# First batch's feed-forward inputs made one tile per attention group and fetched from DRAM, in a two-block adaLN kernel

## The reference, cut to what matters

```
x [4 batches, 512 rows, 512]                       two adaLN blocks
block 0: x = x + ga*attn0(ln(x)*(1+ca)+sa);  x = x + gb*ffn0(ln(x)*(1+cb)+sb)
block 1: x = x + ga*attn1(ln(x)*(1+ca)+sa)         <- "attention groups"
           attn1: 32 query heads of 128, 8 key/value heads, causal in windows of the
           whole sequence, softmax in f32, then @ w_o (4096 x 512)
         x = x + gb*ffn1(h), h = ln(x)*(1+cb)+sb    <- "last stage"
           ffn1(h) = down( silu(gate(h)) * up(h) ), hidden width 1792 = 14 chunks of 128
ln(v) = (v - mean(v)) / sqrt(var(v) + 1e-5), along the last axis (512)
```

## Time and profile before

| | us |
|---|---|
| median of 3 runs | 1852.1 |
| profiled execution, its own time | 1854.24 |
| its span, first to last instruction | 1852.5 |
| PE busy | 1807.5 (98%) |
| DVE busy | 1283.4 (69%) |
| ACT busy | 1123.1 (61%) |
| POOL busy | 448.1 (24%) |
| mean granted TensorE clock | 0.992 |

### The profile page before, as it was taken

One profiled execution on the slowest core, in us unless ns is written; L12 is line 12 of the kernel. 1 busy time (PEld: TensorE's weight loads), 2 busy tenths in 40 slices (PEclk: granted clock), 3 DMA queues, 4 the chain that ended last, 5 costly groups with the idle time before them and its releaser, 6 DMA issues.

```text
span 1852.5 us, 29061 instructions
## 1 busy us (share of the span) xinstructions
PE 1807.5 (98%) x8863; PEld 1508.2 (81%) x8863; DVE 1283.4 (69%) x3032; ACT 1123.1 (61%) x2620; POOL 448.1 (24%) x429
## 2 busy tenths in 40 slices
PE   6998999999999999999999999999999989999999
PEld 4566788888888888888888888888888867888887
DVE  6897677877767676766777777777777785544442
ACT  5755766667667676766666676666666673333331
POOL 2234404041323224041612123140313132010000
PEclk9899999999999999999999999999999999999999
DMA  9026567666766776776776778677777767313010
GB/s 347 2 80 224 157 191 216 203 192 191 204 200 194 211 200 198 205 231 207 214 211 197 208 202 226 191 217 212 197 213 203 210 186 243 109 57 114 27 41 23
DMA packets 239368, 331.25 MB, mean 179 GB/s; under 512 B 26008, under 2 KB 165528, under 8 KB 238880
## 3 DMA queue, kind: packets, MB, share of 16 engines
q1 hardware_dynamic: 238736, 328.93, 59.6%
q10 hardware_dynamic: 528, 1.05, 0.2%
HBM read 200.39 MB, written 129.50 MB: 178 GB/s over the span
## 4 chain that ended last, share of the span: by engine, by line
PE 79%; DVE 7%; DMA 6%; ACT 4%; SPq 2%; issue 2%; DVEq 0%; ACTq 0%
PE ps L2073 23%; PE ps L2139 15%; PE ps L2264 11%; PE ps L2121 9%; PE ps L2106 9%; PE ps L2246 5%; DMA turned_blocks<-tp 4%; ACT probs L2362 2%; PE ps L2125 1%; PE ps L2103 1%; SPq L1779 1%; PE ps L1245 1%; DMA pd<-turned_blocks 1%; DVE pt L2628 1%; DVE stats L864 1%
## 5 line engine op out<-in xcount | busy, mean ns | idle before, releaser
L2073 PE MATMUL ps<-hA,wq 128*128 128x512 f32 x1536 | 385.8, 400 | 0.0
L2139 PE MATMUL ps<-wo,oT 128*128 128x512 f32 x1536 | 367.2, 390 | 3.7 <-issue 2.3
L2139 PEld LDWEIGHTS ps<-wo,oT 128*128 128x128 f32 x1536 | 287.8, 188 | 64.3 <-issue 3.1
L2604 DVE CUSTOM_DVE_ANT_0 ps<-ps,mask 128x512 f32<-128x512 f32 (+3 forms) x512 | 235.8, 523 | 143.5 <-PE ps L2106 142.9
L2381 ACT ACTIVATE pt<-pd 128x1280 fp32r<-128x1280 f32 x128 | 163.0, 1273 | 272.2 <-PE ps L2121 231.3
L2073 PEld LDWEIGHTS ps<-hA,wq 128*128 128x128 f32 x1536 | 279.0, 188 | 56.4 <-issue 0.2
L2362 ACT ACTIVATE probs<-ps,nmax 128x512 f32<-128x512 f32 (+3 forms) x512 | 263.1, 532 | 71.3 <-DVE nmax L2604 71.3
L2370 ACT ACTIVATE probs<-probs,rinv 128x512 f32<-128x512 f32 (+3 forms) x512 | 246.2, 552 | 38.3 <-DVE rinv L2610 38.3
L2121 PE MATMUL ps<-pt,V 128*128 128x512 f32 (+2 forms) x1152 | 253.3, 349 | 11.1 <-DVE pt L2628 10.5
L2121 PEld LDWEIGHTS ps<-pt,V 128*128 128x128 f32 x1152 | 196.2, 190 | 40.3 <-issue 15.3
L2106 PE MATMUL ps<-kT,qT 128*128 128x512 f32 (+2 forms) x1152 | 224.7, 340 | 0.0
(11 more groups left out here) (256 smaller groups left out, 2602.3 us busy)
## 6 DMA issues: line engine op xcount, KB each, us to landing
turned_blocks<-tp SPq DMA_DIRECT2D x128, 640.0 KB, 3.5
pd<-turned_blocks SPq DMA_DIRECT2D x512, 160.0 KB, 3.3
wq_next<-in_L_attn_w_q_dram SPq DMA_DIRECT2D x16, 1024.0 KB, 6.5
wo_in<-in_L_attn_w_o_dram SPq DMA_DIRECT2D x15, 1024.0 KB, 8.2
turned_weights<-hf_chunk SPq DMA_DIRECT2D x168, 64.0 KB, 2.6
wm<-in_L_wmod_dram SPq DMA_DIRECT2D x4, 2048.0 KB, 13.5
turned_values<-tv SPq DMA_DIRECT2D x32, 256.0 KB, 3.2
xh_m<-turned_weights SPq DMA_DIRECT2D x28, 256.0 KB, 3.7
```

Source lines behind the costliest of these rows:

```text
L2073: last = nc.tensor.matmul(ps[:, bank, :], w[i][:, c, cols], hT[k][:, c, b * S:(b + 1) * S], start=(c == 0 and n == 0), stop=(c == DC - 1 a ...
L2139: last = nc.tensor.matmul(ps[:, bank, :], oT[x_][:, b, h, r * P:(r + 1) * P], wo[y_][:, h, :], start=(h == 0 and n == 0), stop=(h == GQ - ...
L2604: nc.vector.tensor_tensor_reduce(out=v, in0=v, in1=mask[:, TB * P - KEYS[i]:], scale=-1.0, scalar=3e38, op0=ALU.add, op1=ALU.min, accum_ou ...
```

## The change

The preparation of batch 0 leaves group 15. In groups 9 to 12, one tile of 128 rows in each, SP loads x and attention of the tile (unit 0), POOL adds them, SP stores the sum to `attended` (unit 1), DVE makes the statistics (unit 2), POOL takes the inverse root with 14 small chained instructions and normalises (in front of its second split of q weights), DVE transposes (unit 4), the bounce goes through DRAM (units 4 and 5), ACT modulates and rounds (unit 6), DVE makes the low part (unit 7), and SP stores both parts to `first_inputs` in DRAM. In group 15 SP loads these into `fT` (units 1, 6, 7), and in flush the sum into `xt[:, 0]`. The loop over groups is cut in two. PE's 16 transposes, ACT's eight modulations, its square root and the table exchange, POOL's copies and DVE's four low parts are gone from group 15 and flush. `gate_up(0, 0)` moves in front of `outputs(g, -1)` and `gate_up(0, 1)` behind it; `place_wide(0)` moves into unit 7 and `place_wide(1)` in front of `p_low(g, -1)`.

```diff
-                    with eng.Fori(NKV + 1, NG - 1) as g:
+                    with eng.Fori(NKV + 1, NKV + 1 + TB) as g:
+                        body(g, False, True, True)
+                    with eng.Fori(NKV + 1 + TB, NG - 1) as g:
                         body(g, False, True)
...                                                          SP: new helpers
+                        def load_ahead(g):
+                            sp.dma_start(hp_f[0], tile_view(mid_t, g)).then_inc(ld_x[PAIR], 16)
+                            sp.dma_start(hp_f[1], tile_view(att_t, g)).then_inc(ld_x[PAIR], 16)
+                        def store_sum(g):
+                            sp.wait_ge(s["root"], ROOT_STEPS * ahead_job(g) + 1)
+                            sp.dma_start(tile_view(att_t, g), hp_f[0]).then_inc(stored, 16)
+                        def store_ahead_turned(g):
+                            sp.wait_ge(n_turned, ahead_job(g) + (AHEAD_JOBS + 1))
+                            sp.dma_start(rows_d.rearrange("a j b x -> (a j) (b x)"), hp_f[1]).then_inc(n_bounced, 16)
+                        def load_ahead_turned(g):
+                            sp.wait_ge(n_bounced, 16 * ahead_job(g) + 16 * (AHEAD_JOBS + 1))
+                            for b_ in range(NQD):
+                                sp.dma_start(hp_f[0][QD * b_:QD * (b_ + 1), :]..., rows_d[:, :, b_, :]...)
+                        def store_ahead(g):
+                            sp.wait_ge(n_lo, ahead_job(g) + (AHEAD_JOBS + 1))
+                            for k in range(2):
+                                sp.dma_start(first_d[k]..., hp_f[k]...).then_inc(later_stored, 16)
+                        def load_first(k, chunks):
+                            sp.dma_start(fT[k][:, chunks, :].bitcast(F32), first_d[k, chunks]...) \
+                                .then_inc(ld_at_first, 16)
...                                                          SP: body
-                                if not more and u < 2:
+                                if not more and u == 1:
                                     sp.wait_ge(wq_split, GQ * NG)
-                                    ...
-                                    sp.dma_start(x_first[:, two, :], mid_t[0][:, two, :])
-                                    for t in range(2):
-                                        sp.dma_start(at_first[t], att_t[0][:, 2 * u + t, :])
+                                    sp.wait_ge(later_stored, 32 * (AHEAD_JOBS + TB))
+                                    load_first(0, slice(1, DC))
+                                    load_first(1, slice(0, 2))
                                 if not more and u >= 6:
                                     for q in range(2 * (u - 6), 2 * (u - 6) + 2):
                                         load_turned(sp, q)
+                                if not more and u == 6:
+                                    load_first(1, slice(2, DC))
+                                if not more and u == 7:
+                                    load_first(0, slice(0, 1))
+                                if ahead and u == 0:
+                                    load_ahead(g)
+                                if ahead and u == 1:
+                                    store_sum(g)
+                                if ahead and u == 4:
+                                    store_ahead_turned(g)
+                                if ahead and u == 5:
+                                    load_ahead_turned(g)
+                                if ahead and u == 7:
+                                    store_ahead(g)
...                                                          SP: flush, behind gsc, usc, dsc
+                            sp.wait_ge(q_full, UNITS * NG)
+                            sp.wait_ge(v_full, PAIR * NG)
+                            sp.dma_start(xt[:, 0], att_t[0]).then_inc(s["x0"], 16)
                             sp.wait_ge(s["w_kept"], 16 * NQD * TILES + 16)
                             next_weights(4)
                             next_weights(5)
...                                                          POOL: normal_ahead, between next_q(0) and next_q(1)
+                            pool.wait_ge(s["agg"], k + 1)
+                            then(nc.gpsimd.tensor_scalar(var, mv_f[:, 0, 1:2], EPS, None, ALU.add))
+                            then(nc.gpsimd.tensor_scalar(root.bitcast(I32), var.bitcast(I32), -0.5, ROOT_SEED, ...))
+                            for _ in range(4):
+                                then(nc.gpsimd.tensor_scalar(step, root, var, root, ALU.mult, ALU.mult))
+                                then(nc.gpsimd.tensor_scalar(step, step, -0.5, 1.5, ALU.mult, ALU.add))
+                                then(nc.gpsimd.tensor_tensor(root, root, step, ALU.mult))
+                            nc.gpsimd.tensor_scalar(hp_f[0], hp_f[0], mv_f[:, 0, 0:1], root, ALU.subtract, ALU.mult)
...                                                          PE
                         def gate_up(n, j, first):
-                            if j == 0:
-                                pe.wait_ge(s["lo"], DC * n + (DC + 2))
+                            if first and j == 0:
+                                pe.wait_ge(ld_at_first, 64)
+                                pe.wait_ge(exp_done, UNITS * TB * NG + TB)
...                                                          PE: flush
                             outputs(g, -2)
-                            pe.wait_ge(s["hi"], DC + 1)
-                            turn(xt[:, 1], range(3, DC))
                             out_project(g - 1, 3)
+                            gate_up(0, 0, True)
                             outputs(g, -1)
+                            gate_up(0, 1, True)
                             out_project(g - 1, 4)
-                            gate_up(0, 0, True)
                             out_project(g - 1, 5)
-                            gate_up(0, 1, True)
                             out_project(g - 1, 6)
                             out_project(g - 1, 7)
...                                                          ACT: body, unit 6, behind p_high
+                                if ahead and u == 6:
+                                    modulate_ahead(g)
...                                                          (four activations of 128x128 and a copy of 128x512)
-                                if last and u == 4:
-                                    root(0)
-                                    nc.scalar.activation(rstd_2[:, TB:TB + 1], rstd_2[:, TB:TB + 1], ACT.Exp, scale=0.0)
...                                                          DVE: body, at the end of the units
-                                if last and u == 6:
-                                    normal(0, lambda t: x_first[:, t, :], xt[:, 1])
-                                if last and u in (2, 3):
-                                    statistics_first(2 * u - 4)
-                                    statistics_first(2 * u - 3)
-                                if last and u == 3:
-                                    variances(0)
+                                if ahead and u == 2:
+                                    statistics_ahead(g)
+                                if ahead and u == 4:
+                                    turn_ahead(g)
+                                if ahead and u == 7:
+                                    low_ahead(g)
+                                if last and u == 7:
+                                    dve.wait_ge(wo_split, GQ * NG)
+                                    place_wide(0)
...                                                          DVE: flush
                             p_low(g, -2)
                             o_low(g, -3)
-                            dve.wait_ge(wo_split, GQ * g)
-                            place_wide(0)
                             add_out(g - 1, 2)
-                            lows(0, range(2))
                             o_low(g, -2)
+                            place_wide(1)
                             p_low(g, -1)
                             add_out(g - 1, 3)
-                            lows(0, range(2, DC))
                             o_low(g, -1)
-                            place_wide(1)
                             add_out(g - 1, 4)
```

170 lines of the change are left out of this document (101 added, 69 removed).

## The result

| | kernel before | changed kernel |
|---|---|---|
| median, us | 1851.8 (4 runs, 1851.4 to 1853.2) | 1877.3 (4 runs, 1874.5 to 1881.0) |
| ratio | 1 | 1.0135 [1.0119, 1.0150] |
| profiled execution, us (span) | 1854.24 (1852.5) | 1874.49 (1872.8) |

The change makes the kernel 25 us slower. I had forecast 7.4 slower and a range that ended at 1867. The profiled execution is the fastest of the changed kernel's four, so its stretches account for 20.3 of the 25 us; where the rest goes isn't shown.

The account below looks back on a forecast made before the run. PE, busy 98% of the span, was taken to bound the kernel. Marker +3.3 us (group 15's gains against flush's wait for tile 4) plus 4.2 in groups 9 to 12 made +7.5: 1859.5, range 1850 to 1867.

Parts of the forecast that it names:

- the gaps that were to stay: Group 15: PE's gap of 1.58 before out_project(0) stays at about 1.7; a wait of 1.05 replaces the transposes before outputs(5).
- (d): Group 15, before outputs(5): removing twelve transposes (1.5 us) exposes a PE wait of 1.05, so the gain is 0.3 to 0.45.
- (b): Group 15, unit 5: the 3.06 gap shrinks by 2.2, 1.5 from ACT's root and table load, 0.7 from DVE's slowed p_low.
- (a): Group 15, unit 3: the 0.75 gap, put down to DVE's statistics and POOL's addition, goes entirely.
- the 5 to 8 that I had named: Flush, sign that the forecast is right: outputs(7) idles 5 to 8 us, ended by DVE's pt.
- the 3.7 for tile 4: Flush: 1.25 MB in front on SP's queue delays weight tile 4 by 3.7 us, so it lands at 1529.5.
- Rival 1: Flush: xt's 1 MB drains beside tile 4 without holding it; marker 3.9 us earlier, time 1848.2; chance 0.12.
- Groups 9 to 12 ... Sum 4 x 1.05 = +4.2 us: Inner groups: work added on ACT and SP costs 1.05 us a group, 4.2 in all, with bounds 0 and 12.
- Loss 0.55 a group: Groups 9 to 12: ACT's added 2.2 us in unit 6 exceeds the slack of 1.63 before outputs(5), costing 0.55 a group.
- I take half of that, 0.5 a group: Groups 9 to 12: unit 0's 0.5 MB makes SP lag; priced at half of group 9's gaps of 0.69 and 0.32.
- The steps at nothing: Inner groups: POOL's 14 small operations and normalisation, DVE's four additions and the second loop cost PE nothing.
- Rival 3: Groups 9 to 12: SP's lag reaches further, 2.5 us a group, 10 + 3.3 in all, time 1865.4; chance 0.1.

Follow-up runs that it names:

- e7: Kernel before with only batch 0's reciprocal root made on POOL, in place of ACT's root and table loads in group 15; ratio 0.9991.
- e11: The same kernel as e7, measured again to narrow its interval; ratio 0.9979.
- e8: e7 with gate_up(0, 0) put in front of out_project(4) and gate_up(0, 1) in front of out_project(5); ratio 0.9992 to the kernel before.
- e2: Changed kernel with the 1 MB load of xt put behind weight tiles 4 and 5 on SP's queue; ratio 1.0165 to the kernel before.
- e4: Changed kernel with ACT's modulation in groups 9 to 12 cut to one chunk of four, work left out; ratio 1.0132 to the kernel before.
- e6: Changed kernel with unit 0's loads cut to 16 of 512 columns and ACT's modulation to one chunk of four; ratio 1.0092 to the kernel before.
- e3: Changed kernel with unit 0's loads in groups 9 to 12 cut to 16 of 512 columns; ratio 1.0162 to the kernel before.
- e13: e6 with POOL's reciprocal root also cut from 14 small operations to 2; ratio 1.0104 to the kernel before.
- e14: e6 with the transfers of units 1, 4 and 5 cut too (stored sum, turned tile and its loads); ratio 1.0065 to the kernel before.
- e15: e13 and e14 together, with DVE's subtraction of unit 7 cut to 128 of 512 columns; ratio 1.0058 to the kernel before.

## Why the prediction was wrong in size

**Right: what bounds it, and group 15.** The marker carried everything (304.4 us from it to the end before, 304.5 after). Forecast -4.2 up to scores(15, 7), measured -4.4; the gaps that were to stay stayed (1.62 for 1.7; 1.04 for 1.05 in (d)). The Trainium skill, "ScalarE: Activation LUTs", section "What ACT_TABLE_LOAD costs", would have made (b) 2.4 us larger with its drain of 1.38 us; e7 and e11, which take the exchange away alone, win 4.2 and 4.4 with the slow clock that followed the gap (e8 wins 2.5), so the sum from the rows stands and the drain doesn't show. One reason in it isn't borne out: (a) put the gap of 0.75 down to statistics and additions, which e7 and e11 keep, and it is gone in both, and 0.94 in e8. What makes it is not shown.

**Right in kind, short in size: flush.** The mechanism was the forecast one. gate_up(0, 0) waits 3.7 (3.0), tile 4 lands 16.6 us after the pd load (15.5), outputs(7) starts 30.8 us behind scores(15, 7) (29.3), and the wait for DVE before the marker grew by 1.3 and not 0.8. Together +10.2 for +7.5. The store of tp in unit 7 took 4.9 behind the 0.5 MB, where 2.92 + 1.3 is 4.2; the 1514.0 at which I let it land is 0.3 more than these terms add up to. The gap before outputs(7) is 4.80 and not 6.6, just under the 5 to 8 that I had named, because gate_up(0, 0) ran slow for 1.9 of it. That the 3.7 for tile 4 came near the 4.8 measured is in part luck: its queue part is 2.6 (4.1 for 1 MB in the row), and the other 2.3 is a later issue by SP, for which the sum had no term. Rival 1, that 1 MB doesn't hold tile 4, is refuted by e2. The rule of ring order ("DMA: Bandwidth & Descriptors", section "Queues, rings and completion order", in the Trainium skill) agrees in kind. The 2.9 us that the prediction estimated from the page's rate, for 1.25 MB, are nearer to the 2.6 measured than the 3.7 taken from the row; 0.25 MB of them (load_first) had landed 0.6 us before tile 4 was issued.

**Wrong: "Groups 9 to 12 ... Sum 4 x 1.05 = +4.2 us".** Measured 18.4 in the profiled execution, 18.4 to 26.5 over the four with the same inner code, above my upper bound of 12. The profiled sum missed by 12.8: this term by 14.2 and flush by 2.7, with 4.2 of noise ahead of group 9 the other way. Two of its steps failed.
- "Loss 0.55 a group" for ACT. I took the added 2.2 from a slack of 1.63 that holds when the rest is on time. Measured: 1.7 a group in unit 7 (up to 3.1 in the kernels with the same inner code). The gaps themselves are 0.5 to 2.0 in the changed kernel, at most the 2.2 added, and where more was lost, slow matmuls followed the gap. e4 and e6 show that ACT's work is the cause. In group 11, where SP was on time again, the gap was the forecast 0.5.
- "I take half of that, 0.5 a group" for SP's lag. I had the mechanism (tp's store held by loads in front, 7 us for 3 to 4) and saw 6.3 and 8.2, but priced its end by the small gaps of group 9, as if lateness were spent once. It isn't: tp's store, pd's load, p_high, p_low and outputs are a chain from unit to unit. A late SP issues its next load (wq_next, 1 MB) directly in front of the next store, so the lag grows, and by the gaps of unit 7 the slack that would hide ACT's work is what the lag has used up. This last link is read from the timelines, and e3 speaks against it in part: with small loads unit 7 still lost 9.6. No run has all transfers small and the modulation whole, which would show what ACT costs by itself. With both cut the groups still lost 7.7 (16.3 in e13), and 1.4 and 4.0 once the other transfers were small too. And a gap can cost twice: the slow matmuls behind the 1.97 made 3.8 of it. I had priced the clock in flush and at nothing in the inner groups.

The steps at nothing held where SP was on time, in e14 and by e15's median: POOL's 14 operations, DVE's additions, the second loop. Where DVE is already late they stand in the way: the statistics in front of the maxima, and p_low beside POOL, 1.0 longer in group 11. Rival 3 (2.5 a group) named the right mechanism, at a chance of 0.1 and half of its size.

What stays open: why executions with the same inner code differ by up to 8 us in these groups, where the last 4 to 8 us of e14 and e15 go, and whether a placement exists in which the tiles cost nothing there. Two that I tried did not find one.

## What to carry to other kernels

A stretch in which the bounding engine has no gap can still have next to no slack: find the chain that feeds it (here a store and a load through DRAM in every unit) and count every byte that the change puts in front of it on its queue, and also the large loads that a late queue would issue directly in front of it. Where several delays were added, cutting one may show nothing in the time: here only two cuts together did. Before moving work out of a gap, take away the one instruction that makes the gap: the root alone won all that the whole move won in group 15, in two of three profiled executions. An instruction in an in-order queue that waits for something nobody needs yet delays everything behind it, whatever its own size.
